# Feed-forward of a two-layer gated block: the row chain a quarter of a tile earlier, the down products a quarter later, and a new order in VectorE's queue

## The reference, cut to what matters

```python
def rmsnorm(x, weight, eps=EPS):
    return x * jax.lax.rsqrt(jnp.mean(x * x, axis=-1, keepdims=True) + eps) * weight
def activation_quant(x):
    scale = 127.0 / jnp.clip(jnp.max(jnp.abs(x), axis=-1, keepdims=True), 1e-05, None)
    return jnp.clip(jnp.round(x * scale), -128, 127) / scale
def bitlinear(x, w):                      # H = 512, F = 1408
    return jnp.einsum('bsh,oh->bso', activation_quant(x), weight_quant(w))
...
gate, up = jnp.split(bitlinear(rmsnorm(x, norm_weight), w_gate_up), 2, axis=-1)
hidden = jnp.square(jax.nn.relu(gate)) * up
x = x + jnp.tanh(g_ffn[1]) * bitlinear(hidden, w_down)     # x inside is layernormed first
```

## Time and profile before

| | before |
|---|---|
| median of 3 runs | 3264.98 us (3264.69 to 3271.52) |
| the profiled execution's own time | 3268.12 us |
| its span, first to last instruction | 3266.4 us |
| mean granted TensorE clock | 0.966 |
| busy over the whole span | PE 90%, DVE 73%, ACT 64%, POOL 42% |
| products of the feed-forward (L3122), first to last start | 3090.9 to 3248.8 us |
| last instruction of DVE (L3236) | starts 3261.49 us |

### The profile page before, as it was taken

The page is one execution under the profiler, slowest core; times in us unless marked ns, Lnnn a source line. Parts: engine busy times, 40 slices in busy tenths (PEclk is TensorE's granted clock), DMA queues, the critical chain, the costliest instruction groups (busy, mean ns, idle before and its releaser), DMA issues. The chain is left out here.

```text
span 3266.4 us, 57053 instructions
## 1 busy us (share of the span) xinstructions
PE 2954.8 (90%) x15542; PEld 2350.4 (72%) x15542; DVE 2395.4 (73%) x4800; ACT 2100.0 (64%) x4303; POOL 1362.4 (42%) x1689
## 2 busy tenths in 40 slices
PE   6849889788899969979999899999999999899887
PEld 4636666577788847758888778888888888688644
DVE  6849999865676757776676269999999999735376
ACT  3448888431566635556666488888888888533365
POOL 3402000313000038336666267777777777441122
PEclk9979999899899979989999999999999999999999
DMA  5787654213888749875656632333223232286300
GB/s 187 246 180 178 152 146 123 84 46 136 281 267 267 232 140 311 209 183 150 191 157 194 216 90 86 95 97 95 77 87 95 95 96 70 95 284 213 111 24 30
DMA packets 410911, 491.10 MB, mean 150 GB/s; under 512 B 36788, under 2 KB 268116, under 8 KB 410740
## 3 DMA queue, kind: packets, MB, share of 16 engines
q1 hardware_dynamic: 397780, 436.50, 45.1%
q0 software_dynamic: 12960, 52.61, 4.7%
HBM read 312.69 MB, written 176.31 MB: 150 GB/s over the span
## 5 line engine op out<-in xcount | busy, mean ns | idle before, releaser
L2798 POOL TENSOR_SCALAR h_probs<-h_exp,h_rowsum_inv 128x512 f32<-128x512 f32 x512 | 355.9, 695 | 274.7 <-PE h_pT L2646 258.5
L2726 DVE TENSOR_REDUCE h_neg_max<-h_scores 128x1 f32<-128x512 f32 x512 | 349.4, 682 | 141.2 <-PE h_scores L2638 141.0
L2688 ACT ACTIVATE h_exp<-h_scores,h_neg_max 128x512 f32<-128x512 f32 x512 | 355.7, 695 | 108.7 <-DVE h_neg_max L2726 100.3
L2739 DVE TENSOR_TENSOR h_probsT_lo<-h_pT,h_probsT_hi 128x512 fp32r<-128x512 f32 x512 | 348.4, 681 | 0.0
L2646 PE MATMUL h_pT<-ident,h_probs 128*128 128x128 f32 x2048 | 306.1, 271 | 0.9 <-POOL h_probs L2798 0.8
L2646 PEld LDWEIGHTS h_pT<-ident,h_probs 128*128 128x128 f32 x2048 | 252.7, 139 | 69.9 <-POOL h_probs L2798 1.8
L2697 ACT CAST h_probsT_hi<-h_pT 128x512 fp32r<-128x512 f32 x512 | 300.9, 588 | 0.9 <-PE h_pT L2646 0.9
L2914 PE MATMUL k_acc<-k_w_hi,k_cat 128*128 128x512 f32 x512 | 201.0, 392 | 11.8 <-POOL k_w_lo L2995 10.9
L857 ACT ACTIVATE b_probs<-b_scores,b_neg_max 128x512 f32<-128x512 f32 x256 | 180.4, 705 | 40.1 <-DVE b_neg_max L885 39.8
L885 DVE TENSOR_REDUCE b_neg_max<-b_scores 128x1 f32<-128x512 f32 x256 | 174.0, 680 | 38.9 <-PE b_scores L808 38.9
L2661 PE MATMUL h_pO<-h_probsT_hi,n_lo 128*128 128x512 f32 x512 | 201.2, 393 | 0.0
(11 more groups left out here) (439 smaller groups left out, 9113.1 us busy)
## 6 DMA issues: line engine op xcount, KB each, us to landing
e_w_raw<-in_w SPq DMA_DIRECT2D x24, 1792.0 KB
lnT<-g_out SPq DMA_DIRECT2D x160, 256.0 KB
n_raw<-lnT SPq DMA_DIRECT2D x64, 512.0 KB, 5.2
e_w_raw<-in_w SPq DMA_DIRECT2D x24, 896.0 KB, 9.9
b_q_stack<-qk SPq DMA_DIRECT2D x64, 256.0 KB
b_k_stack<-qk SPq DMA_DIRECT2D x64, 256.0 KB
xq<-f_out SPq DMA_DIRECT2D x16, 1024.0 KB
n_raw<-lnT SPq DMA_DIRECT2D x64, 256.0 KB, 5.4
```

The lines of the kernel that those rows point to most:

```text
L2688: nc.scalar.activation(Pr[:, r % 4], pS[r % 2][:], ACT.Exp, bias=nmax[:, r % 4:r % 4 + 1], accum_out=rsum[:, r % 4:r % 4 + 1]).then_inc(ex ...
L2726: v.tensor_reduce(nmax[:, r % 4:r % 4 + 1], pS[r % 2][:], axis=AX, op=ALU.max, negate=True).then_inc(nmax_done.sem, 1)
L2739: v.tensor_tensor(PTl[:, br * HPG + h, :, bass.ts(q, P)], pT[r % 4][:], PTh[:, br * HPG + h, :, bass.ts(q, P)], ALU.subtract).then_inc(lo_ ...
L2798: nc.gpsimd.tensor_scalar(Pn[:, r % 4], Pr[:, r % 4], rinv[:, r % 4:r % 4 + 1], 1.0, ALU.mult, ALU.mult).then_inc(norm_done.sem, 1)
```

## The change

Only the four tables of lags and orders are changed, those of PE, ACT, DVE and POOL; no instruction is added or taken out. The tables, before and after:

```diff
PE
-        pipeline(pe, N, N, [(gate_up, 9), (down_part, 16), (at(3, h_transposes), 12), (at(3, x_transposes), 5)])
+        pipeline(pe, N, N, [(at(3, h_transposes), 13), (gate_up, 9), (down_part, 17), (at(3, x_transposes), 4)])
ACT
-        pipeline(act, N, N, [(at(3, qT_copy), 13), (relu_square, 9), (at(3, hT_copy), 5), (at(3, centre), 1)])
+        pipeline(act, N, N, [(at(3, qT_copy), 13), (relu_square, 9), (at(3, hT_copy), 4), (at(3, centre), 0)])
DVE
-        pipeline(dve, N, N, [(at(3, hidden_scale), 10), (at(3, hidden_round), 11), (at(3, hidden_int), 12),
-                             (at(3, residual), 17), (at(3, round_add), 4), (at(3, round_sub), 5), (at(3, scale), 3),
-                             (hidden, 9)])
+        pipeline(dve, N, N, [(at(3, residual), 17), (at(3, hidden_scale), 10), (at(3, hidden_round), 11), (at(3, hidden_int), 12),
+                             (at(3, round_add), 3), (at(3, round_sub), 4), (hidden, 9), (at(3, scale), 1)])
POOL
-        pipeline(pool, N, N, [(at(3, weigh), 2), (at(3, cubes), 3), (at(3, out_factor), 11)])
+        pipeline(pool, N, N, [(at(3, weigh), 1), (at(3, cubes), 2), (at(3, out_factor), 11)])
```

## The result

| | before | after |
|---|---|---|
| median of 6 runs | 3266.65 us (3263.30 to 3271.52) | 3275.99 us (3273.76 to 3279.62) |
| ratio | | 1.0027, 95% interval 1.0017 to 1.0038 |
| the profiled execution's own time | 3268.12 us | 3277.60 us |
| span, mean granted clock | 3266.4 us, 0.966 | 3275.8 us, 0.966 |
| start of the first product of the feed-forward (L3122) | 3090.86 us | 3086.51 us |

The kernel is slower, by 9.3 us by the medians. The stage itself is 13.6 us longer in this pair of profiles: the stages ahead of it, which hold no changed line, happened to end 4.4 us earlier in the changed kernel's. The last experiment comes back to both.

The account below looks back on a forecast made before the run. No engine is full; the longest closed loop of queue orders and semaphores sets the row. +13.2 for 14 loops, +0.6 start, -1.0 into row 15, 0 tail: +12.8 us, forecasting 3277.8 us (+0.39%) for the median, range 3273 to 3284.

Parts of the forecast that it names:

- the loop of 11.0 us: Steady-state row: DVE's 7.05 us plus 3.96 over PE and ACT replace 10.07, 0.94 us more a row; 87 in 100.
- The waits of PE that go: PE, each row: waits of 0.68 and 0.29 us go, and that of 0.59 shrinks or goes.
- DVE's run: DVE, from a row's last `hidden` until PE sees `round_sub`: an unbroken run of 7.05 us.
- The two new waits: PE, each row: about 1.8 us ahead of quarter 2's products, 0.5 to 1.0 ahead of the row's transposes.
- PE and ACT's part: From the start of the row's transposes over ACT's copies, `centre`, relu and square to the last `hidden`: 3.96 us.
- The residual: DVE, ahead of the last `hidden`: over at 3.8 us, before the square at 3.96, so it costs nothing.
- POOL: `weigh` costs nothing; `cubes` moves beside `hidden_round`, bounded at 0 to 0.19 us a row, taken as 0.
- The sum: Whole kernel: 14 loops +13.2 us, start +0.6, way into row 15 -1.0, tail 0; total +12.8 us.
- The way into row 15: Last loop, into row 15: no further row to scale, so 0.98 us falls out, -1.0 us.
- that nothing would take the place of PE's waits: Rival: PE runs through at 8.5 us a row, 1.56 less, -23 us over 15 rows, 3242 us; 4 in 100.
- A row as long as before: Rival: a row takes 10.1 to 10.4 us, kernel 3265 to 3270 us, within 0.2%; 7 in 100.
- the clock: Rival: PE's longer waits drop its clock to 1.2 GHz, its 8.5 us become 17, some 3368 us; 2 in 100.

Follow-up runs that it names:

- The last experiment: Both kernels timed again unchanged: the kernel before against itself, ratio 0.9998; the changed kernel 3282.01 us against 3268.09, ratio 1.0042.
- experiment 6: Changed kernel with the row's largest magnitude taken over 8 of 512 columns, quantisation partly left out: 10.44 us a row, 3269.28 us.
- experiment 2: Kernel of experiment 1 (`centre` first in ACT's table) plus a wait holding POOL's `weigh` until `hidden_int` of row n-3 is done: 10.40 us a row, 3271.43 us.
- Experiment 4: Changed kernel with DVE's residual behind the last `hidden` instead of ahead of it: 11.63 us a row, 3290.96 us.
- experiment 1: Changed kernel with `centre` moved to the front of ACT's table, out of its run of copies: 11.32 us a row, 3284.83 us.
- experiment 8: Changed kernel with PE, ACT and DVE tables reordered, `round_add` and `round_sub` ahead of `hidden_scale`, `scale` later: 8.45 us a row, 3242.97 us against the kernel before's 3270.69.
- experiment 5: Changed kernel with ACT's table as before the change (`hT_copy` lag 5, `centre` lag 1): 12.50 us in the rows that are alike, 3306.81 us.

## Why the prediction was right

It gave 3277.8 us and a range of 3273 to 3284; the median is 3276.0. The steps below, read from one profile of each kernel, bear out the loop of 11.0 us; that the median comes within 2 us is in part luck. The forecast was 12.8 us more, the medians of the first comparison differ by 9.3 and those of the second by 13.9, and the two medians of the changed kernel, 3276.0 and 3282.0, lie 6 us apart. By its steps, in the order in which it gave them, with the changed kernel's trace:

- **The waits of PE that go.** Right: none of the three is left.
- **DVE's run.** 7.05 us forecast, 7.02 measured. The step that stood in no row, `hidden_scale`'s last to `hidden`, taken as 0.13 between 0.08 and 0.21 (the middle that it names would be 0.145), is 0.13 (3166.26 to 3166.39). That the maximum of `scale`, 0.68 of its 0.98 us, counts in full is shown by experiment 6, for the 0.53 us that it takes out.
- **The two new waits.** 1.8 and 0.5 to 1.0 us forecast, 1.61 and 0.81 measured.
- **PE and ACT's part.** 3.96 forecast, 3.95 measured. `centre`'s step, taken as 0.73 between 0.70 and 0.84, is 0.72. That ACT is in the loop is shown by experiment 2, where taking `centre` out gains 0.57 us; from there on the residual holds the last `hidden`.
- **The residual.** Forecast at nothing, and it is so: it ends at 3162.24, and `hidden` waits 0.51 us more, for ACT. The forecast saw only 0.2 us of room, since it went by bounds. Experiment 4 shows the price of the other place.
- **POOL.** The second instruction of `cubes`, not the third, falls beside `hidden_round`; it takes 0.93 us and `hidden_round` keeps its 0.95. POOL gave way again, as assumed. The 0.19 us that DVE might have lost did not come; but experiment 1 shows that the price is real where `weigh` comes first, and there it is 0.92.
- **The sum.** From the last `hidden` of row 0 to that of row 14 it is 153.6 us against 140.8: +12.8 for 13.2 forecast. The first of these intervals took 11.63 us, 0.7 more than the others (9.92 in the kernel before, 0.15 less than its others), and the last only 10.40, since no further row is centred: the 0.57 us of experiment 2 again. The start cost +0.8 (forecast 0.6). The tail was forecast at 0 and cost 1.0 us, as the timeline of PE shows there: the hidden layer's transposes ran at the lower clock, 1.35 us for the 0.79 of the earlier trace rows, and the last down products waited for the residual of the row before.

```profile
3263.36 1.35 PE L3130 MATMUL k_pT<-ident,k_hidden_int 128*128 128x128 bf16 x11 [2.54 <-DVE k_hidden_int L3230]
...
3266.51 4.22 PE L3141 MATMUL k_down<-k_w_down,k_qT 128*128 128x512 bf16 x11 [0.94 <-DVE k_x L3236]
```

That is the clock and not the order. In the second profile of the changed kernel these transposes took 0.79 us, the down products waited for their copies instead, and the tail was 11.4 us from the last `hidden` to the last residual; in the second of the kernel before it was 12.2. The first pair had them the other way round, 12.2 and 11.2.

- **The way into row 15.** It gained 1.0 us as forecast, 8.60 us against 9.65, but not as the prediction works it out, so this agreement is luck. `scale` has no further row in either kernel, so its 0.98 us fall out of both; the loop of 11.0 less 0.98 is 10.0, which against 9.65 would be 0.4 more. The prediction left out that the changed loop loses more there: with no `scale`, `round_add` and `round_sub` DVE's run is 5.45 us instead of 7.02, and with no row's transposes, copy and `centre` the part over PE and ACT is 3.15 instead of 3.95. Together that is the 8.60.

In all +13.6 us for the stage in the first pair of profiles and +11.3 in the second, against 12.8 forecast.

The rivals: that nothing would take the place of PE's waits was wrong for this order, though experiment 8 shows that another order of the same instructions comes within 0.05 us a row of it. A row as long as before needed 0.6 us that were not there. Of the rows between the start of the stage and the tail the clock fell in one alone, the second: the transposes of the hidden layer took 1.38 us there behind waits of 2.29 and 1.46 us. The 0.7 us of the first interval go with it: in the second profile, where the slow stretch was longer (a mean clock of 0.63 over 9.3 us, against 0.82 in the first), that interval is 12.25 us. The prediction gave the clock little chance because of a wait of 1.70 us without a fall; the second profile of the kernel before has the same wait with one, so that argument does not carry, though its conclusion held for the steady state. Its price was too high as well: down products took 1.84 times as long at the lower level in experiment 5 (1.49 us for 0.81), which makes 15.6 us of PE's 8.5, by estimate, and not 17.

Where the expected gain went: each wait of PE was removed, but another loop, longer than the one whose waits went, now sets the row. The prediction never traced the loop of 10.07 us that it replaces. It can be walked in the earlier trace rows and these two lines of the kernel before:

```profile
3162.32 0.46 ACT L3158 ACTIVATE k_relu<-k_gate 128x352 f32<-128x352 f32 x1 [0.75 <-PE k_up L3122]
3162.81 0.50 ACT L3161 ACTIVATE k_relu<-k_relu 128x352 f32<-128x352 f32 x1
```

From the hidden layer's transposes (3166.99) it goes over their copies (3167.81, 3168.72), the first down part (3169.26), the row's transposes (3169.92), their copy (3170.34) and the next row's first products (3170.98); then, in the lines of one row earlier, relu (3162.32), square (3162.81), `hidden` of quarter 0 (3163.34), `hidden_round`, `scale`, `hidden` of quarter 1 and `hidden_int` (3166.04) back to the transposes (3166.99). Each of these either waits for the one ahead of it or stands right behind it in its queue. So `scale` stood in the loop before, too. What the changed loop has and the old one had not is the large maximum with the small ones behind it (2.10 us), the last `hidden`, `round_add` and `round_sub` on DVE, and `centre` on ACT; what it lost are the hidden layer's transposes, the first down part and the first quarter's products on PE. This is read from the trace; no experiment was made on the kernel before.

## What to carry to other kernels

With in-order queues, no engine full and the same pattern in each row, look for the closed loop: walk from an instruction over queues and semaphores back to the same instruction one row later, and add the steps from the trace. Giving an operation more lead on one engine is free only if its new place lies outside the longest such loop, and a removed wait says nothing by itself: here the row went from 10.07 to 10.97 us with three waits gone and two new ones in their place, and to 8.45 with the same work in another order. Before an input is made early, ask which engine's work starts earlier with it and what that collides with.

## What the runs showed of the hardware that was not expected

A POOL product of 128x512 that starts 0.20 us ahead of a DVE conversion of 128x1408 held it back: 1.81 us instead of 0.89, in each row of the steady state of experiment 1 alike. TensorE's clock went to its lower level again and again in experiment 5, where a row at full clock has PE busy for 8.5 of 12.5 us, with waits of 1.24, 1.95 and 0.81 us (0.61, 1.35 and 1.49 us for work that takes 0.40, 0.79 and 0.81 at full clock). In the steady state of the changed kernel, 8.5 of 10.97 us with waits of 1.61 and 0.81, it did so in neither profile, and not in experiment 1 either, 11.32 us a row with waits of 1.25 and 1.74. And the same wait of 1.70 us in the same kernel had the lower level behind it in one profile and not in the other, so one execution without a fall does not show that a wait is borne. The Trainium skill (TensorE: Matmul & The Clock Gate, the section on a second failure mode of the gate) speaks of many short gaps that make the clock swing; the rows of experiment 5 agree with it, and those of the changed kernel show that such gaps need not do so.
